# Cross-attention and a mixture of experts on one core: every engine's order laid anew, x kept on chip, and no repeated products ahead of the scores

## The reference

```python
x = x + xattn(layernorm(x), ctx, ctx)      # x: 16 x 128 x 256, ctx: 16 x 128 x 64
x = x + ffn(layernorm(x), gate, w1, w2, w3)

def xattn(q, k, v):                        # 32 query heads, 8 key/value heads, head size 8
    scores = einsum('bkgsd,bktd->bkgst', q, k) / sqrt(8)
    return einsum('bkgst,bktd->bkgsd', softmax(scores), v)

def ffn(x, ...):                           # 8 experts, 512 wide, the best 2 for each of 2048 tokens
    probs = softmax(x @ gate.T); w, idx = top_k(probs, 2); w = w / w.sum()
    y[e] = (silu(x @ w1[e].T) * (x @ w3[e].T)) @ w2[e].T
    return sum over the two chosen experts of w * y[e]
```

## Time and profile before

| | |
|---|---|
| median of 3 runs | 503.43 us (502.18 to 504.77) |
| the profiled execution's own time | 502.8 us |
| its span, first to last instruction | 501.0 us |
| mean granted TensorE clock | 0.892 |
| first stage, to the first product of a tile of the experts | 281.8 us |
| second stage, 39 tiles | some 219 us |

### The profile page before, as it was taken

How to read it: one execution, slowest core, us unless ns; L and a number is a source line. 1 busy time by engine, 2 the same in 40 slices (tenths; PEclk the granted TensorE clock), 3 DMA queues, 4 the chain that set the end, 5 groups by cost and what they waited for, 6 DMA issues and landing times.

```text
span 501.0 us, 8509 instructions
## 1 busy us (share of the span) xinstructions
PE 378.0 (75%) x2233; PEld 264.8 (53%) x2256; DVE 247.6 (49%) x718; ACT 195.4 (39%) x395; POOL 177.0 (35%) x298
## 2 busy tenths in 40 slices
PE   0155968677868586859351499999999999999990
PEld 0033434334544343433131378888888888888870
DVE  7757848574848485845268532323223232332320
ACT  3213748445646555556544123232232322323220
POOL 9330025065443425261754013232232323323231
PEclk9998979895969988975855599999999999999996
DMA  6465777886785777421115122323333232332311
GB/s 208 112 108 116 180 181 194 207 211 173 199 215 171 207 183 216 107 86 33 69 50 179 42 43 43 54 53 53 53 44 55 48 53 53 51 54 43 43 21 21
DMA packets 47598, 52.99 MB, mean 106 GB/s; under 512 B 18640, under 2 KB 40272, under 8 KB 47568
## 3 DMA queue, kind: packets, MB, share of 16 engines
q1 hardware_dynamic: 39264, 42.00, 32.4%
q0 software_dynamic: 7152, 9.34, 11.8%
q10 hardware_dynamic: 1152, 1.29, 0.8%
HBM read 32.66 MB, written 17.47 MB: 100 GB/s over the span
## 4 chain that ended last, share of the span: by engine, by line
PE 55%; DVE 13%; POOL 9%; issue 8%; DMA 8%; ACT 3%; SPq 1%; ACTq 0%; another core or an unknown queue 0%; POOLq 0%; DVEq 0%
PE bank L716 22%; PE bank L734 13%; POOL slots_d L436 5%; DMA qst<-negT 5%; PE bank L726 3%; PE bank L597 3%; PE bank L584 3%; PE bank L630 2%; DVE wlo L1065 2%; PE bank L561 2%; PE bank L704 2%; DVE negm L994 2%; PE bank L558 1%; DVE identb L1111 1%; DVE stat L939 1%
## 5 line engine op out<-in xcount | busy, mean ns | idle before, releaser
L524 POOL DMA_INDIRECT out_rows<-ys,meta x39 | 60.6, 1555 | 159.6 <-DVE ys L1247 157.1
L994 DVE TENSOR_REDUCE negm<-bank 128x4 f32<-128x512 f32 x128 | 84.6, 680 | 53.3 <-PE bank L561 52.1
L775 ACT ACTIVATE prob<-bank 128x512 f32<-128x512 f32 x128 | 75.9, 597 | 64.3 <-PE bank L584 45.2
L1240 DVE TENSOR_TENSOR gat<-bank,sil 128x512 f32<-128x512 f32 x39 | 27.0, 692 | 112.5 <-PE bank L716 112.5
L734 PE MATMUL bank<-w,gT 128*128 x312 | 73.9, 380 | 0.8 <-ACT gT L917 0.8
L584 PE MATMUL bank<-qst,kst 128*128 128x512 bf16 x106 | 46.3, 442 | 32.4 <-ACT prob L775 25.4
L911 ACT ACTIVATE sil<-bank 128x512 f32<-128x512 f32 x39 | 23.3, 599 | 105.8 <-PE bank L716 105.8
L716 PE MATMUL bank<-whi,xhi 128*128 x156 | 60.3, 468 | 1.2 <-ACT xhi L905 1.2
L734 PEld LDWEIGHTS bank<-w,gT 128*128 128x128 f32 x312 | 56.3, 190 | 7.1 <-issue 1.0
L561 PEld LDWEIGHTS bank<-kst,qst 125*128 125x128 bf16 x512 | 43.9, 107 | 30.0 <-issue 10.5
L561 PE MATMUL bank<-kst,qst 125*128 125x128 bf16 x512 | 54.5, 236 | 0.3
(11 more groups left out here) (119 smaller groups left out, 515.9 us busy)
## 6 DMA issues: line engine op xcount, KB each, us to landing
xs<-slots_d SPq DMA_DIRECT2D x39, 129.0 KB, 2.0
w<-in_w1T SPq DMA_DIRECT2D x8, 512.0 KB, 6.6
w<-in_w3T SPq DMA_DIRECT2D x8, 512.0 KB, 6.7
w<-in_w2T SPq DMA_DIRECT2D x8, 512.0 KB
qparts_d<-qp SPq DMA_DIRECT2D x16, 192.0 KB, 3.6
qst<-qparts_d SPq DMA_DIRECT2D x16, 192.0 KB
xin<-in_x SPq DMA_DIRECT2D x16, 128.0 KB, 4.4
qst<-qparts_d SPq DMA_DIRECT2D x16, 128.0 KB
```

Of the source, the lines that this page charges most:

```text
L524: pool.indirect_dma_start(out, IndirectOffsetOnAxis(ap=meta[:, r4, 0:1].bitcast(I32), axis=0), ys[:, r4, :], None, compute_op=ALU.add).the ...
L775: act.activation(prob[:, k, :], ps_e[k % 2][:, :], ACT.Exp, scale=SCALE).then_inc(exp_done, 1)
L994: dve.tensor_reduce(negm[:, b % 2, g * G:(g + 1) * G], ps_s[(8 * b + g) % 3][:, :].rearrange("p (h t) -> p h t", h=G), AX.X, ALU.max, nega ...
L1240: dve.tensor_tensor(gat[:, u, :], ps_h3[u][:, :], sil, ALU.mult).then_inc(g_done, 1)
```

## The change

Three things change at once. The six repeated products of each batch are left out (`FILL` is all zero; 96 products of 512 columns in all). x is held on chip: batches 0 to 7 in `xin`, batches 8 to 15 in `xin2`, the last part of the buffer of w3; `add_res` reads batches 0 to 7 from there, and `load_res` is kept for 8 to 15 only. And every engine's list is written in a new order, partly with new buffers: a third `slot` buffer, the keys stored as three parts (`kparts_d`), batch 0's keys laid straight from the chip (`first_k`), the casts of the constants on ACT, and the clearing of `qst` in four parts.

```diff
-FILL = (1, 0, 1, 1, 1, 0, 1, 1)
+FILL = (0,) * KV
...
+        xin2 = w13[:, 1, E * KC * F - XR * D:].rearrange("p (b d) -> p b d", b=XR)
...
-        slot = sb1("slot", [P, 2, 2 * TOPK], I32)
+        slot = sb1("slot", [P, 3, 2 * TOPK], I32)
...
+            def first_k(j):
+                if j == 0:
+                    sp.wait_ge(const_b, 2)
+                sp.wait_ge(k_split, (1, 3, 4)[j])
+                first, n = K_RUNS[j]
+                for t in range(first, first + n):
+                    sp.dma_start(kst[t * HD:(t + 1) * HD, 0, :], kp[0:HD, j, :]).then_inc(kst_in[0], 16)
...
-                pool.tensor_tensor(x2[:, b % 2, :], att[:, :], xres[:, b % 2, :], ALU.add).then_inc(x2_ready, 1)
+                pool.tensor_tensor(x2[:, b % 2, :], att[:, :], xin[:, b, :] if b < XR else xres[:, b % 2, :], ALU.add).then_inc(x2_ready, 1)
...
-                if i % 2 == 0 and i >= 4:
+                if i % 2 == 1 and 0 <= i - 5 < B - 2:
+                    scatter((i - 5) // 2, 0)
+                if i % 2 == 0 and 0 <= i - 4 < B - 2:
                     add_seen((i - 4) // 2)
                 if 0 <= i - 1 < B:
                     add_res(i - 1)
-                if i % 2 == 0 and i >= 4:
-                    scatter((i - 4) // 2)
...
+                if i % 2 == 1 and 0 <= i - 5 < B - 2:
+                    scatter((i - 5) // 2, 1)
...
+                if 3 <= i + 5 < B:
+                    q_transpose(i + 5, max(2, min(i + 4, B - 1)), min(i + 1, B - 1), (i - 5) // 2)
...
+            split_hi(15)
+            split_hi(16)
...
+            split_hi(24)
+            copy_x2T(7)
```

More of the change, by code:

```diff
@@ L883, in _ @@
[L883 to L898 removed]
+                if i >= 0:
+                    exps(i, 0)
@@ new lines, in _ @@
+                if 0 <= i - 1 < B:
+                    copy_oT(i - 1)
+                if i >= 0:
+                    exps(i, 3)
+                if 0 <= i + 1 < B:
+                    copy_negT(i + 1)
+                if i == 15:
+                    split_hi(9)
+                if i >= 0:
+                    exps(i, 4)
+                if i % 2 == 1 and 0 <= i - 3 < B - 2:
+                    normal2(i - 3)
+                if i >= 0:
+                    exps(i, 5)
+                if i % 2 == 0 and 0 <= i - 4 < B - 2:
+                    weight_exp((i - 4) // 2)
@@ new lines, in _ @@
+                if i % 2 == 1 and 0 <= i - 3 < B - 2:
+                    copy_x2T((i - 3) // 2)
+                if i == 15:
+                    split_hi(11)
+                if i == 14:
+                    split_hi(7)
+            split_hi(12)
+            copy_oT(15)
+            split_hi(13)
+            split_hi(14)
+            normal2(14)
+            weight_exp(6)
+            split_hi(15)
+            split_hi(16)
+            split_hi(17)
+            split_hi(18)
+            split_hi(19)
@@ L901, in copy_xhi @@
+            split_hi(20)
+            split_hi(21)
+            split_hi(22)
+            split_hi(23)
+            split_hi(24)
+            copy_x2T(7)
+            normal2(15)
+            weight_exp(7)
+            split_hi(25)
+            split_hi(26)
+            split_hi(27)
+            split_hi(28)
+            split_hi(29)
+            copy_x2T(8)
+            split_hi(30)
+            split_hi(31)
+            weight_exp(8)
             def copy_xhi(j, u):
@@ new lines, in _ @@
+            split_lo(11)
+            read_logits(6)
+            split_lo(12)
+            choose(6)
+            mark(6)
+            normalise(15, 0)
+            split_lo(13)
+            normalise(15, 1)
+            weigh(6)
+            split_lo(14)
+            stats2(15)
+            guess_unit(8)
+            root_last()
+            split_lo(16)
+            place(6)
+            read_logits(7)
+            choose(7)
+            weigh(7)
+            mark(7)
+            split_lo(17)
```

720 lines of the change are left out of this document (434 added, 286 removed).

## The result

The changed kernel takes 460.74 us (median of 4 runs, 459.57 to 462.49) against 502.81 us of the kernel before on the same chip. The ratio is 0.9176, with a 95% interval of 0.911 to 0.9241: 42 us less. The forecast was 451 us, with a range of 437 to 480.

A forecast was written before the change was run, and what follows sets the result against it. The first stage's rounds were taken as bound by waits (POOL's root, negT's transfer), not an engine's throughput. Terms -40, -7, -7 and +2 sum to -52 us, from 502.8 to 451 us; range of 8 in 10: 437 to 480.

The forecast's parts named there:

- rival 1: The forecast itself: first-stage rounds of about 10 us, giving 440 to 462 us in all; chance 0.55.
- Rounds: Fourteen distances between negT copies, with the root's wait gone: 141.4 us for 181.6, -40 us, bounds -24 to -51.
- about 4 us: In each round, the time from its first product to the start of negT's copy, behind half of ACT's work.
- the granted clock near 1 from round 3 on: Sign expected in the profile: PE's granted clock stands near 1 from round 3 on.
- no turn of short and long: Sign expected in the rounds: starts of negT's copies lie 9.3 to 11 us apart, without short and long alternating.
- The start: Before the first rounds: constants cast on ACT and clearing in four parts bring the query's store earlier; -7 us, bounds -3, -9.
- The last rounds: From the last negT copy to the copy of oT: a 5.85 us wait for the root goes; -7 us, bounds -4, -10.
- The end: End of the first stage: ACT's high parts hold up the last two units' logits and the table; +2 us, bounds 0, +4.
- The repeated products: Six products a round on PE, 1.3 us: removing them gives nothing directly and could cost only through the clock.
- The rival beside it: PE's clock stays low without repeats in all rounds: 521 us, chance 0.04; in part of them 472 to 484, chance 0.1.
- x on chip: Takes 128 KB of transfers from eight rounds; nothing on the critical way waits for it, so no time was counted.
- Rival 2: Transfers set the rounds, negT landing late in each round with weights: 158 us for the rounds, 470 in all; chance 0.22.

The follow-up runs named there:

- the run with three edits: Changed kernel with w2 loaded late, first stage's end reordered (last weight ahead of six splits), POOL's round 6 root behind the query's last step: 451.91 us.

## Why the prediction was right, and where it was off

The time lies in the range and the forecast's rival 1 came true, 9.7 us above its value. That it lies so near owes something to luck: the rounds missed by 8.7 us and the end by 7.7, and the last rounds (3.9 us better than their term) and the experts (2.8 us, in no term) paid part of it back. Point by point:

**Rounds, -40 us predicted, -31.3 measured.** The mechanism held: the wait at `normal2` is gone from the rounds, and in eleven of them PE now waits for negT. The total is inside my bounds (-24 to -51). One reading of mine was loose: the 11.1 us in 5 times of the earlier trace rows are the weight load's wait (PEld) for negT; PE's own at that line was 6.6 us in 4 times. The whole miss is in the twelve rounds with weights, 131.6 us together, 11.0 each, for my 10.2; the last two make 18.6 for my 19.0. In the eleven that wait, the first product of a batch starts 3.4 to 7.7 us after the issue of its negT, 5.7 in the mean (in the chain 3.2 to 6.2; the two longest, 6.8 and 7.7, are those that end at 134.55 and 158.14). I had 4.9 to 6.8, so the middle held and the ends did not. Mis-sized is the other piece of that way, "about 4 us" from the first product to the copy of negT. It takes 3.86 to 6.38 us, 4.9 in the mean. Two things that I left out of it are in that: the eight products of the logits, which stand there in every second round (4.76 us for 3.86, both at a granted clock of 1.00), and the low clock in six of the eleven. I expected "the granted clock near 1 from round 3 on"; it is 0.91 over the rounds. And "no turn of short and long" was half right: the distances lie between 7.6 and 13.2 us. Behind the longest stands the transfer of 7.7 us; SP issued it at once, as it did in all but one of the sixteen cases (0.8 us late at 106.95). No run shows what makes some of these transfers twice as long as others. In three rounds PE does not wait for negT at all; one of these is among the long ones (12.3 us), and there it waits for DVE's maxima.

**The start, -7 predicted, -7.2 measured.** The first copies of negT stand at 34.35 and 41.62 for 48.81 of negT(1), the first exponential at 38.51 (I said 39). The mechanism held at its beginning, the number partly by luck. The store of the first query came 6.6 us earlier (13.17 for 19.79), and PE's wait in front of the first scores shrank to 1.12 us. But the first copy of negT is only 3.8 us earlier (34.35 for 38.17), since its turning now stands behind the fourth score group of batch 1, and PE waited 4.82 us for that batch's query, until 31.17. The rest came from a place that I had counted for the rounds alone: negT was issued at once and not 2.0 us behind its copy, and took 3.16 us for 4.92.

**The last rounds, -7 predicted, -10.9 measured**, from the last copy of negT to that of oT, which came at 205.37 (I said 201, for the rounds' sake). It is just outside my bound of -10, but half of it was only lent, as the sum of batch 14 shows: to there it is -5.2. The kernel with the scatter alone has -6.5 here, so having the scatter out of the root's way is most of it, as I had put it down.

**The end, +2 predicted with bounds 0 and +4, +9.7 measured.** This is the mis-sized term, and I had named it as one that would make me wrong. Some 5.7 us of it are the other side of the last rounds; from the sum of batch 14 on it is +4.0. The two terms together, -5 in my sum, measured -1.2. I had priced ACT's ten splits and taken half of them as covered by the root "on DVE". That was right for rows 15 alone. For rows 14 it was POOL that was late: their root started at 208.43, behind a split and two indirect transfers, where before it had ended by the time that oT(15) was copied. And the sum of batch 15, whose input DVE had written at 209.36, came on POOL behind the root, the tokens, a split that itself waited for ACT, and the marks, at 216.20. With both mended the first product stands 36.4 us after the end of the sum of batch 14 instead of 37.6 (239.62 - 203.18, 242.05 - 204.49), so that most of the +4.0 stayed. How much of the rest the last weight was, which only the run with three edits moved, was not taken apart.

**The repeated products, in no term.** This was right, and is shown in both orders: +2.0 us with them in the new order (the intervals overlap), and a ratio of 0.9994 without them in the old. The rule of the Trainium skill that I had named (TensorE: Matmul & The Clock Gate, "HAM oscillation", that idle stretches between bursts bring the clock down) agrees with the trace in the main: 0.50 after a wait of 3.14 us, though 1.00 after one of 2.75. The rival beside it fell, since the clock goes down behind waits that are there with and without the repeats: over the rounds it is 0.93 with the repeats and 0.91 without, at the same time.

**x on chip, in no term.** This was right within what can be measured: without it 2.7 us more by the medians and 1.3 by the ratios, with intervals that overlap.

**Rival 2, transfers that set the rounds (470 us).** This is half a truth. The wait for negT's transfer is PE's longest in the rounds, and their share of 0.77 is as high as before. But 512 KB more in each of twelve rounds made the kernel 5.1 us slower by the medians and 2.7 by the ratios, not clear of the uncertainty; the order and the moment of issue are worth 17 us (negT from ACT's queue) and 46 us (negT ahead of the query).

## What to carry to other kernels

When two waits on one round trip take turns, taking one away shows the other: moving the scatter alone gave 12 us, all moves together 42. Before moving an instruction on an engine or a queue, list for every consumer all the semaphores it waits for, not just the one that the profile names: `normal2` waited for a root and for a scatter, and mending the one by delaying the other gave nothing. An engine that stands waiting in front of a transfer may be what keeps bulk transfers from running ahead of a small one on which everything hangs, and the transfers behind the wait must still be early enough for their own readers.

## What the runs showed of the hardware

- A transfer of 24 KB that was issued at once from another queue, with bulk ahead of it or beside it, landed later (5.0 to 11.7 us in the chain) than one that SP issued with most of the bulk held behind it (3.2 to 6.2 us in the chain, 7.7 at the longest up to PE's first use). The cause is argued, not shown.
- The same stretch of PE's list takes 3.86 us at a granted clock of 1.00 and 5.77 us at 0.50. The low one stood behind six of seven waits of PE for negT of 2.1 to 4.1 us and behind none of four of 0.6 to 1.6 us. The six repeats in each batch did not change the time by what could be measured.
- 512 KB more from DRAM to DRAM in each of twelve rounds cost 0.2 us each by the ratios and 0.5 by the profile, which is not clear of the uncertainty, though the transfer engines' share was already 0.77; it rose to 0.82.
